# Fewer rows for a head's q and k, and matmuls of zeros beside the third head's scores

## What is computed

```python
B, H, W, C = 4, 16, 16, 192;  NH = 12;  HD = 16;  WS = 14
qkv = xw @ qkv_w + qkv_b                       # xw: layer-normed windows of 14 x 14 tokens
rel_h = jnp.einsum('bhwc,hkc->bhwk', rq, Rh)
rel_w = jnp.einsum('bhwc,wkc->bhwk', rq, Rw)
scores = jnp.einsum('bqd,bkd->bqk', q, k) * SCALE + bias
attn = jax.nn.softmax(scores, axis=-1)
o = jnp.einsum('bqk,bkd->bqd', attn, v)
```

## Time and profile before

| what | value |
|---|---|
| median of 3 runs | 190.46 us (189.41 to 191.38) |
| the profiled execution | 190.22 us |
| its span, first to last instruction | 188.4 us |
| TensorE matmuls busy | 175.3 us (93%), 1502 |
| VectorE busy | 112.9 us (60%), 303 |
| ScalarE busy | 87.5 us (46%), 230 |
| GpSimd busy | 65.7 us (35%), 120 |
| mean granted TensorE clock | 0.991 |
| DMA | 12958 packets, 19.45 MB, mean 103 GB/s |

### The profile page before, as it was taken

How to read it: one execution, slowest core, us unless ns; L and a number is a source line. 1 busy time by engine, 2 the same in 40 slices (tenths; PEclk the granted TensorE clock), 3 DMA queues, 4 the chain that set the end, 5 groups by cost and what they waited for, 6 DMA issues and landing times.

```text
span 188.4 us, 4169 instructions
## 1 busy us (share of the span) xinstructions
PE 175.3 (93%) x1502; PEld 153.3 (81%) x1502; DVE 112.9 (60%) x303; ACT 87.5 (46%) x230; POOL 65.7 (35%) x120
## 2 busy tenths in 40 slices
PE   7999999997998797899999999999999999999892
PEld 7766996696786675788877996878999999789892
DVE  6729675598888677587755776520111466779532
ACT  3496554934387666587785204554100223071300
POOL 1633439936055456431999521900000000000000
PEclk9999999999699999999999999999999999999999
DMA  5791227976939999957051300000012170000015
GB/s 161 210 221 25 89 79 205 225 204 180 185 105 187 218 213 205 209 115 239 12 155 41 129 0 0 0 3 0 3 43 83 42 171 0 2 0 3 0 31 138
DMA packets 12958, 19.45 MB, mean 103 GB/s; under 512 B 5197, under 2 KB 9695, under 8 KB 12938
## 3 DMA queue, kind: packets, MB, share of 16 engines
q0 software_dynamic: 3392, 10.98, 24.4%
q1 hardware_dynamic: 8810, 7.75, 17.5%
q10 hardware_dynamic: 736, 0.46, 0.9%
HBM read 6.79 MB, written 1.57 MB: 44 GB/s over the span
## 4 chain that ended last, share of the span: by engine, by line
PE 70%; DMA 9%; DVE 7%; SPq 5%; ACT 3%; issue 2%; POOL 0%; ACTq 0%; DVEq 0%; POOLq 0%
PE bank L1632 9%; PE bank L1649 8%; PE bank L1406 6%; PE bank L1474 5%; PE bank L1667 4%; DMA qop<-arena 4%; PE bank L1392 3%; SPq L607 3%; PE bank L1381 3%; PE bank L1488 3%; PE bank L1600 3%; DMA q_last<-maxt 3%; PE bank L1659 3%; PE bank L1446 3%; DMA xt<-in_x_tok 2%
## 5 line engine op out<-in xcount | busy, mean ns | idle before, releaser
L1190 DVE TENSOR_REDUCE negmax<-bank 98x2 f32<-98x392 f32 (+1 forms) x72 | 34.7, 525 | 8.8 <-PE bank L1446 8.7
L1474 PE MATMUL bank<-qop,kop 128*98 128x196 f32 (+4 forms) x140 | 22.6, 262 | 0.1
L951 ACT ACTIVATE arena<-bank 98x392 f32<-98x392 f32 x48 | 21.2, 489 | 2.5 <-PE bank L1474 2.2
L1446 PE MATMUL bank<-kop,qop 126*98 126x196 f32 x80 | 16.4, 294 | 5.3 <-DMA qop<-arena 3.8
L1474 PEld LDWEIGHTS bank<-qop,kop 128*98 128x98 f32 (+4 forms) x140 | 18.8, 176 | 0.9 <-issue 0.9
L1632 PE MATMUL bank<-h2t,wf 96*128 96x512 f32 x72 | 17.4, 398 | 0.4 <-ACT h2t L978 0.4
L1446 PEld LDWEIGHTS bank<-kop,qop 126*98 126x98 f32 x80 | 11.1, 175 | 7.3 <-issue 5.7
L1632 PEld LDWEIGHTS bank<-h2t,wf 96*128 96x128 f32 x72 | 13.3, 188 | 3.9 <-issue 0.6
L1649 PE MATMUL bank<-wf,arena 128*128 128x192 f32 x96 | 15.8, 326 | 0.0
L1649 PEld LDWEIGHTS bank<-wf,arena 128*128 128x128 f32 x96 | 15.7, 190 | 0.1
L1269 DVE TENSOR_TENSOR arena<-bank,arena 128x384 f32<-128x384 f32 x4 | 2.2, 556 | 22.1 <-PE bank L1649 22.1
(11 more groups left out here) (172 smaller groups left out, 379.5 us busy)
## 6 DMA issues: line engine op xcount, KB each, us to landing
kop<-arena POOLq DMA_DIRECT2D x20, 173.0 KB, 5.5
qop<-arena POOLq DMA_DIRECT2D x10, 227.5 KB, 6.7
qop<-arena SPq DMA_DIRECT2D x10, 130.0 KB, 2.5
qop<-arena POOLq DMA_DIRECT2D x10, 130.0 KB, 6.0
arena<-in_relw SPq DMA_DIRECT2D x2, 441.0 KB, 5.1
xt<-in_x_tok SPq DMA_DIRECT2D x4, 192.0 KB, 3.5
scratch<-arena SPq DMA_DIRECT2D x4, 192.0 KB, 2.0
k_last<-arena POOLq DMA_DIRECT2D x4, 173.0 KB, 4.8
```

Of the source, the lines that this page charges most:

```text
L951: nc.scalar.activation(pg[:, e], src[0:HWIN, 0:2 * WIN], ACT.Exp, scale=HD ** -0.5).then_inc(emptied(key), 1)
L1190: nc.vector.tensor_reduce(negmax[0:rows, n % 2, at:at + cols], ps(key)[0:rows, 0:cols * width].rearrange("p (t k) -> p t k", t=cols), AX.X ...
L1446: ins = mm(ps(key)[0:HWIN, WIN * t:WIN * t + WIN], qo(h)[0:126, c0:c0 + HWIN], ko(h)[0:126, WIN * u:WIN * u + WIN], start=True, stop=True)
L1474: ins = mm(ps(key)[0:rows, at:at + n], ko(h)[:, c0:c0 + rows], rhs, start=True, stop=True)
```

## The change

It drops the product of ql and kl: rows 32 to 47 hold ql once, against kh once, and rows 48 to 63 are zeros in all buffers. GpSimd sets 16 partitions of `k2` to zero at the start (`blank`, a place that is later overwritten), SyncE copies them into rows 48 to 63 of the five buffers of q and of k, and at h = 1 from the first buffer into the sixth. TensorE waits for the copies ahead of the heads. Beside this, TensorE multiplies two passes of zeros ahead of each of S(2, 3), S(2, 4) and S(2, 5), into the bank of the maxima.

```diff
+        blank = k2[0:16, 1, 1]
         def q_rows(h, part):
             f, j = h // HH, h % HH
-            src = q2[j:j + HH * (HD - 1) + 1:HH, f, part, None, :].to_broadcast([HD, 2, QN])
-            return raw(qo(h)[32 * part:32 * part + 32]), raw(src)
+            if part == 0:
+                src = q2[j:j + HH * (HD - 1) + 1:HH, f, 0, None, :].to_broadcast([HD, 2, QN])
+                return raw(qo(h)[0:32]), raw(src)
+            return raw(qo(h)[32:48]), raw(q2[j:j + HH * (HD - 1) + 1:HH, f, 1, :])
...
             sp.dma_start(relw[:, 1], a["relw"][:, 1]).then_inc(relw_in[1], 16)
+            sp.wait_ge(blank_set, 1)
+            sp.dma_start(raw(kop[48:64]), raw(blank[:, None, :].to_broadcast([16, OWN, KN]))).then_inc(blank_in, 16)
+            sp.dma_start(raw(qop[48:64]), raw(blank[:, None, 0:QN].to_broadcast([16, OWN, QN]))).then_inc(blank_in, 16)
...
                     sp.dma_start(raw(k_last[64:128, :]), raw(kop[64:128, 0])).then_inc(krows_set[OWN], 16)
+                    sp.dma_start(raw(k_last[48:64, :]), raw(kop[48:64, 0])).then_inc(krows_set[OWN], 16)
+                    sp.dma_start(raw(q_last[48:64, :]), raw(qop[48:64, 0])).then_inc(qrows_copied, 16)
                     sp.dma_start(raw(q_last[120:126, :]), raw(qop[120:126, 0])).then_inc(qrows_copied, 16)
...
             nc.gpsimd.memset(raw(q2[:, 1, 1, QB + 112:QR]), 0.0).then_inc(set_up, 1)
+            nc.gpsimd.memset(raw(blank), 0.0).then_inc(blank_set, 1)
...
-                for copy in range(2):
-                    pool.dma_start(raw(ko(h)[32 * copy:32 * copy + 32]),
-                                   raw(k2[j:j + HH * (HD - 1) + 1:HH, f])).then_inc(k_loaded[h % NOK], 16)
+                pool.dma_start(raw(ko(h)[0:32]),
+                               raw(k2[j:j + HH * (HD - 1) + 1:HH, f])).then_inc(k_loaded[h % NOK], 16)
+                pool.dma_start(raw(ko(h)[32:48]),
+                               raw(k2[j:j + HH * (HD - 1) + 1:HH, f, 0])).then_inc(k_loaded[h % NOK], 16)
...
             pe.wait_ge(qrows_copied, 16)
+            pe.wait_ge(blank_in, 32)
             for n in range(NH + 3):
                 first = maxima(n) if n < NH else None
                 for u in range(6):
                     m, p = divmod(6 * n + u - E_LAG, 6)
                     if 0 <= m < NH and p == 0:
                         second = shifted(m)
+                    if n == 2 and u >= 3:
+                        pe.wait_ge(*is_free(("mx", 2)))
+                        kept_busy(2, ps(("mx", 2)))
                     if first:
                         next(first)
```

More of the change, by code:

```diff
@@ L449, in build @@
         qrows_copied = sem("qrows_copied")
+        blank_set = sem("blank_set")
+        blank_in = sem("blank_in")
         krows_set = [sem(f"krows_set{i}") for i in range(NOK)]
@@ L1437, in maxima @@
                         if h == OWN:
-                            pe.wait_ge(qrows_copied, 32)
+                            pe.wait_ge(qrows_copied, 48)
                         pe.wait_ge(r_loaded[o], 16 * (h // NOP + 1))
                         pe.wait_ge(k_loaded[h % NOK], 32 * (h // NOK + 1))
-                        pe.wait_ge(krows_set[h % NOK], 16 if h % NOK == OWN else 1)
+                        pe.wait_ge(krows_set[h % NOK], 32 if h % NOK == OWN else 1)
                     pe.wait_ge(*is_free(key))
```

## The result

| | kernel before | changed kernel |
|---|---|---|
| median | 190.38 us (188.19 to 191.41, 6 runs) | 199.94 us (195.85 to 201.12, 6 runs) |
| the profiled execution | 190.22 us | 198.74 us |
| its span | 188.4 us | 196.8 us |
| mean granted TensorE clock | 0.991 | 0.963 |

The forecast was 193.6 us with a range up to 196.3; the result lies above the range. The two copies of zeros are L565 and L566.

The account below looks back on a forecast made before the run. TensorE was taken to set the end nearly everywhere, except around 45 to 49 us and the heads' loads. 190.22 + 3.8 (bv held) + 0 (loads) - 0.4 (clock) = 193.6 us; range 187.0 to 196.3.

Parts of the forecast that it names:

- `bv` held, 5.0 us: At the start, the v bias load lands 5.0 us later behind the zero copies: 4.2 us first, 0.8 second.
- Cover 1.2 us, loss 3.8: First q bank, needed for the last k product: 1.2 us of the v bias delay is covered, 3.8 us lost.
- From there to 41 us TensorE has no pause in which to win them back.: After the first q bank's release: the 3.8 us lost cannot be recovered by TensorE before 41 us.
- Loads of heads, 0: Head loads of q and k: half the bytes into 16 rows at half rate save nothing; bounds 0 to 4.4 us.
- The multiplied zeros, -0.4: At the third head, zeros keep TensorE's clock at 1.00 and win 0.4 us; bounds -0.9 to +0.5 us.
- The memset and the further copies, 0: GpSimd's memset (at most 2.2 us) hides at the start; sixth-buffer copies at 49 us cost nothing, or 0.3 us.
- R1: Head loads take time by bytes: 2.8 us saved, v bias hold costs 1.3, total 188.3 us; chance 0.15.
- R2: At the start, the v bias load is not held by the zero copies: 189.8 us at present load price; chance 0.13.
- R3: At the start, both zero copies are ahead of the v bias load: 196.0 us; chance 0.20.

## Why the prediction was wrong

The direction was right and the place too, but the size was not. The step that failed is the price of the pause: the sum had one term for it, its length, and none for the slower clock behind it, which measured 6.6 us.

- **`bv` held, 5.0 us.** Right: 5.2 to 5.3 us (the waits of VectorE 5.46 and 0.19). Its parts were not: I had put 4.2 us down for the first copy and a quarter of the second. The run with one copy shows the first alone holding `bv` as long. Its 0.443 MB moved at 90 to 105 GB/s, and `bv`'s own packets, 0.09 MB in both, took 41% of the engines from 16 to 18 us where they took 18% of 12 to 14 us before. That the 5.0 came out is partly luck.
- **Cover 1.2 us, loss 3.8.** The pause is 3.27 us. The cover itself was right: TensorE needs the bank at 18.08 us, and VectorE's L1091 ended at 16.78 before, so 1.3. But VectorE's copy of `bv` takes 0.26 us where it took 0.91, so of the 5.16 us by which that copy starts later (20.04 against 14.88) only 4.51 reach the end of L1105 (21.29 against 16.78).
- **"From there to 41 us TensorE has no pause in which to win them back."** Here the prediction failed. The sentence is true, and it treats a pause as time lost once. The pause also lowered TensorE's clock to 0.50, and it stayed there for 13.6 us, although TensorE was never idle in them; that costs 6.6 us, twice the pause. The rows to see it were there: behind the two pauses of 45 to 49 us, of 1.2 and 0.5 us in 2, the clock was at 0.50, and I reckoned with that in the third head, but not where the change itself makes a longer pause. 193.6 + 6.6 is 200.2, against a measured median of 199.94; against the profiled execution, from which the 6.6 is read, it is 1.5 us too much, which are the other terms: 0.53 in the pause, 0.51 in the zeros, 0.62 in the loads, less 0.18.
- **Loads of heads, 0.** Nearly: 0.698 MB a head at 5.17 us per MB are 3.61 us, against 4.08, so 0.47 us a head. By bytes it would have been 0.74, so the price was between the two bounds: an estimate from these numbers, with the other loads at their old rate, gives the copies into 16 rows about 0.7 of the rate of 32. Some 0.62 us reach the heads' pace by S(11,0). The reason, that rows written and not bytes set the rate, is shown by the spread rows. "Neighbouring" was the word that mattered: with gaps between the sixteen rows the queue as a whole is 1.2 times as quick (5.00 against 4.07 us for a MB).
- **The multiplied zeros, -0.4.** The clock did stay at 1.00, as forecast, and in the changed kernel 0.91 us is won by head 4. In the kernel before 0.85 is won by head 4 and nothing reaches the end (ratio 1.001).
- **The memset and the further copies, 0.** TensorE's waits in the heads of the changed kernel name neither. In the kernel with the filled pause it waits 0.7 us for `q_last`, so the cover of the further copies is thin.
- **R1, by bytes:** false. **R2, `bv` not held:** false, with 10.72 us to land. By the Trainium skill (DMA: Bandwidth & Descriptors, section "Queues, rings and completion order") the engines alternate between queues. The trace agrees from 16 to 18 us, where both queues move packets (41% and 47%), but not before, and no run here shows it to help a small load behind a large one of another queue. **R3, both copies ahead:** its 196.0 us was the nearest number, but not its mechanism: with one copy ahead nothing changes, and in the changed kernel `bv` lands 2.3 us before the second copy. It is near by luck, as it prices a longer hold and no clock.

The sum as measured, from one profiled execution to the other: 190.22 + 3.27 (pause) + 6.60 (half clock, as the rest of the 9.87 us at S(0,0)) - 0.91 (zeros, by head 4) - 0.62 (loads, by head 11) + 0.18 (behind) = 198.74 us. It closes because each term is a difference of start times; the names of the last three are my reading.

The range was too narrow for the same reason: all its cases priced the pause at its length. With the clock as a case, R3 and the forecast would each have had a twin some 6 us higher.

## What to carry to other kernels

Where a change puts a pause into TensorE's work, price the pause and then the slower clock behind it, which here cost twice as much (6.6 us behind 3.3) and lasted through matmuls without a gap; look for a bulk copy that is issued ahead of a small load that someone waits for. If the pause can't be removed, matmuls of zeros in it can keep the clock up (here in nine executions of ten); if it can, move the bulk copy. And when a copy writes few rows, choose rows with gaps between them: the same bytes in every second row took the kernel from 189.61 to 186.48 us.

## What was unexpected in the hardware

- The clock stayed at 0.50 for 13.6 us (21.8 to 35.5 us) with TensorE busy 12.00 of 12 us from 22 to 34 us, through 64 matmuls of 96 x 64 and part of the 32 of 192 columns; it was 13.6 us again in the profile of spread rows with early copies and 17.0 with one copy ahead, while behind the pauses at 45 to 49 us it had been some 3.3 us. With the pause filled the same matmuls ran at 1.00, so they do not lower the clock by themselves; what kept it down isn't settled.
- The fall is not certain. All seven executions of the changed kernel and of that with one copy ahead, whose two profiles show pauses of 3.3 us, have low mean clocks (0.949 to 0.966); with spread rows and early copies, where the profile shows 1.7 us, it is two of four; with the 1.1 us left by the filled pause, one of ten (0.957). The kernel before is not free of it: two of its 31 executions beside the experiments have a mean clock of 0.965 (195.58 and 195.66 us), and of these there is no trace. Nor does a fall need a recorded pause: see 123.5 us in the run with one copy ahead.
- The zero copies were quick when spread and early (194 and 207 GB/s), but not when spread and late: in the kernel of 186.48 us they ran at 96 to 126 GB/s from 17 to 24 us, as with neighbouring rows. They read 16 neighbouring rows in both cases. They are hidden there, so I didn't pursue it; it stays open.
